# Boundary to the expert tiles laid out anew: batch 7's scans ahead of other routing, batch 4 scattered first, two tiles multiplied ahead of the last output

## The reference

```python
x = _layernorm(x + rwkv(x))            # time mixing, three projections, scans over time, Wo
x = _layernorm(x + moe(x))             # 8 experts, the 2 best of each token, F = 176
x = _layernorm(x + linear_attention(x))
x = _layernorm(x + ternary_ffn(x))     # hidden size 704

# moe
router_logits = x_flat @ gate_w.T
top_w, sel = jax.lax.top_k(router_logits, 2)
top_w = jax.nn.softmax(top_w, axis=-1)
h = silu(x_e @ gate_proj.T) * (x_e @ up_proj.T)
out = sum over the two experts of top_w * (h @ down_proj.T)
```

## Time and profile before

| | |
|---|---|
| median of 3 executions | 408.02 us (407.43 to 408.28) |
| the profiled execution's own time | 407.56 us |
| its span | 405.7 us |
| PE busy | 365.0 us, 90% of the span, 2426 matmuls |
| PE weight loads busy | 325.6 us (80%) |
| DVE / ACT / POOL busy | 292.5 (72%) / 210.9 (52%) / 139.3 (34%) us |
| mean granted clock of PE | 0.959 |

### The profile page before, as it was taken

The page is one execution under the profiler, slowest core; times in us unless marked ns, Lnnn a source line. Parts: engine busy times, 40 slices in busy tenths (PEclk is TensorE's granted clock), DMA queues, the critical chain, the costliest instruction groups (busy, mean ns, idle before and its releaser), DMA issues.

```text
span 405.7 us, 7764 instructions
## 1 busy us (share of the span) xinstructions
PE 365.0 (90%) x2426; PEld 325.6 (80%) x2426; DVE 292.5 (72%) x747; ACT 210.9 (52%) x484; POOL 139.3 (34%) x234
## 2 busy tenths in 40 slices
PE   6999999999558999999999868899999999999791
PEld 6999889999436876777777656899999999999680
DVE  5699999999964556797543255687979787886642
ACT  7256686677634333355335322656565645645451
POOL 2001077767765510003211076525344340411111
PEclk9999999999769999999999986999999999999987
DMA  7879611111024457433441132102020200000000
GB/s 221 314 242 177 225 59 40 53 54 53 15 93 129 135 204 225 136 108 92 126 134 44 64 90 65 53 2 78 3 79 0 79 27 2 27 1 27 0 27 26
DMA packets 28567, 35.79 MB, mean 88 GB/s; under 512 B 3696, under 2 KB 25712, under 8 KB 28272
## 3 DMA queue, kind: packets, MB, share of 16 engines
q1 hardware_dynamic: 19696, 21.78, 18.5%
q0 software_dynamic: 3072, 8.39, 6.4%
q10 hardware_dynamic: 5760, 5.12, 3.8%
HBM read 22.83 MB, written 12.45 MB: 87 GB/s over the span
## 4 chain that ended last, share of the span: by engine, by line
PE 42%; DVE 33%; issue 8%; ACT 5%; POOL 5%; DMA 4%; SPq 2%; ACTq 0%; POOLq 0%; DVEq 0%
PE bank L413 12%; PE bank L556 10%; PE bank L577 8%; DVE st L1102 4%; PE bank L745 2%; PE bank L690 2%; PE bank L536 2%; PE bank L566 2%; PE bank L423 2%; DVE arena L1185 2%; DVE arena L1163 2%; DVE arena L1574 2%; DVE arena L1567 2%; DMA arena<-in_xT 2%; DVE arena L1476 1%
## 5 line engine op out<-in xcount | busy, mean ns | idle before, releaser
L807 ACT ACTIVATE arena<-bank 128x256 f32<-128x256 f32 (+1 forms) x118 | 45.3, 422 | 43.9 <-PE bank L577 28.4
L1663 POOL TENSOR_TENSOR ve<-mv,eps 128x2 f32<-128x2 f32 x32 | 7.7, 240 | 159.8 <-DVE mv L1106 106.9
L556 PE MATMUL bank<-gu,arena 128*128 x156 | 54.0, 469 | 0.0
L812 ACT ACTIVATE arena<-arena,nm,rs 128x256 f32<-128x256 f32 x48 | 26.2, 596 | 38.5 <-POOL nm L1671 38.4
L1741 POOL DMA_INDIRECT arena<-yg,ypos x32 | 31.1, 973 | 39.0 <-DMA yg<-arena 30.5
L577 PE MATMUL bank<-dn,arena 96*128 x156 | 41.0, 385 | 3.3 <-DVE arena L1352 3.3
L1715 POOL DMA_INDIRECT xg<-x,pos x32 | 36.6, 1145 | 13.8 <-issue 7.3
L1352 DVE COPY arena<-bank 96x256 f32<-96x256 f32 x39 | 16.3, 419 | 34.2 <-PE bank L566 33.8
L577 PEld LDWEIGHTS bank<-dn,arena 96*128 96x128 f32 x156 | 28.7, 190 | 13.1 <-issue 5.0
L413 PE MATMUL bank<-arena 128*128 128x256 f32 (+2 forms) x192 | 34.4, 322 | 4.4 <-ACT arena L807 3.6
L413 PE MATMUL bank<-x_hi,w1q 128*128 128x256 f32 x128 | 36.0, 305 | 1.5 <-ACT x_hi L807 1.5
(11 more groups left out here) (274 smaller groups left out, 1121.7 us busy)
## 6 DMA issues: line engine op xcount, KB each, us to landing
arena<-xg SPq DMA_DIRECT2D x39, 128.0 KB, 2.2
yg<-arena ACTq DMA_DIRECT2D x39, 128.0 KB, 1.7
arena<-in_xT SPq DMA_DIRECT2D x8, 256.0 KB, 5.3
x<-in_x SPq DMA_DIRECT2D x8, 256.0 KB, 4.4
out<-arena SPq DMA_DIRECT2D x8, 256.0 KB, 2.1
gu<-in_w_gate SPq DMA_DIRECT2D x1, 1408.0 KB, 9.2
gu<-in_w_up SPq DMA_DIRECT2D x1, 1408.0 KB, 8.4
dn<-in_w_down SPq DMA_DIRECT2D x11, 128.0 KB, 5.4
```

What stands on the lines that cost most here:

```text
L556: last = pe.matmul(bank[BANK_GU[i % 2]][:, 0:2 * F], xtT[:, i % 2, chunk(k)], w[:, :, k, :, bass.ds(e, 1), :], start=k == 0, stop=k == KC - 1)
L807: return act.activation(dst, src, ACT.Copy)
L812: last = act.activation(dst[:, t, :], src[:, t, :], ACT.Identity, bias=nm[:, i, t:t + 1], scale=rs[:, i, t:t + 1])
```

## The change

It moves work at the boundary on every engine, adds one small DVE instruction in place of a POOL one, and computes batch 5's weights another way. Cut to its core:

```diff
-GATED = B - 2
+GATED = B - 3
 # SP
+            sp.wait_ge(mv_ok[0], B - 2)
             sp.wait_ge(table_ok, 1)
 # PE, a_slot
                 if 0 <= now < B - 1:
                     output(now)
+                if old == FULL_AT - 1:
+                    rank(old)
+                    first_total()
                 if 0 <= new < B:
                     past(pe, gate_ok, new)
                     project(new, 2, halves(3), rp_mm)
-                if 0 <= old < B:
+                if 0 <= old < FULL_AT - 1:
                     rank(old)
-                    if old == FULL_AT - 1:
-                        first_total()
 # PE, boundary
             tile_order(0, bank[7][:, 4 * E:4 * E + 1])
-            turn_x1(B - 3)
-            logits(B - 3)
             tile_rows(0, bank[7][:, 8 * E:8 * E + 2 * FIRST], where1[:, :, :])
             output(B - 2)
-            rank(B - 3)
+            turn_x1(B - 3)
             for i in range(3):
                 experts[i] = expert_of(i)
             turn(0)
+            logits(B - 3)
             turn(1)
             gate_up(0, experts[0])
             turn(2)
+            gate_up(1, experts[1])
+            rank(B - 3)
+            output(B - 1)
+            turn(3)
+            tile(0)
             turn_x1(B - 2)
-            output(B - 1)
+            tile_front(1)
             logits(B - 2)
-            gate_up(1, experts[1])
-            turn(3)
-            tile_front(0)
-            rank(B - 2)
-            tile_back(0)
-            turn_x1(B - 1)
-            tile_front(1)
-            logits(B - 1)
             tile_back(1)
             tile_front(2)
+            rank(B - 2)
+            tile_back(2)
+            turn_x1(B - 1)
+            tile_front(3)
+            logits(B - 1)
+            tile_back(3)
+            tile_front(4)
             rank(B - 1)
...
 # ACT: a_slot leaves out normalise_x1(5); boundary
             exponents_high(B - 1)
+            gate_exponentials(B - 1)
+            normalise_x1(B - 3)
             copy_x1T(B - 3)
-            gate_exponentials(B - 1)
-            odds(B - 3)
             turned(0)
+            turned(1)
             reciprocal(B - 1)
             act.preload_act_table_set("silu_and_others")
-            turned(1)
-            normalise_x1(B - 2)
             turned(2)
-            copy_x1T(B - 2)
             silu(0)
             silu(1)
+            turned(3)
+            gaps(B - 3)
+            normalise_x1(B - 2)
+            tile(0)
+            copy_x1T(B - 2)
+            tile(1)
             gaps(B - 2)
-            turned(3)
+            tile(2)
             normalise_x1(B - 1)
-            tile(0)
             copy_x1T(B - 1)
-            tile(1)
+            tile(3)
             gaps(B - 1)
-            tile(2)
-            tile(3)
 # DVE, a_slot
                     residual(now)
+                if old == FULL_AT - 1:
+                    positions(old)
+                    dve.wait_ge(pos_ok, old)
+                    dve.wait_ge(route_step, 4 * old + 4)
+                    dve.tensor_copy(pos[:, tiles_of(old), :], pos_f[:, tiles_of(old), :]).then_inc(pos_ok, 1)
+                    first_places()
                 outputs(s)
-                if 0 <= old:
+                if 0 <= old < FULL_AT - 1:
                     positions(old)
 # DVE, boundary
             exponents(B - 1)
-            finish_y(B - 2)
             dve.wait_ge(asked_ok, valid_at[0])
             tile_places(0, where1, bank[7][:, 4 * E:4 * E + 1])
+            differences(B - 1)
+            tile_table(0, bank[7][:, 8 * E:8 * E + 2 * FIRST])
+            finish_y(B - 2)
             states(B - 1)
-            tile_table(0, bank[7][:, 8 * E:8 * E + 2 * FIRST])
+            outputs(B - 1)
             choose(B - 3)
-            residual(B - 2)
-            outputs(B - 1)
-            positions(B - 3)
 # POOL
             for s in range(B + 2):
+                if s - 2 == FULL_AT - 1:
+                    scatter(s - 2)
+                    deviation(0, s)
+                    weights(s - 2)
+                    continue
```

More of the change, by code:

```diff
@@ L626, in _ @@
             pe.matmul(bank[5][:, 0:E], ones[:, :], taken_e[:, :], start=True, stop=True).then_inc(looked_ok, 1)
-            tile_back(2)
-            tile_front(3)
+            tile_back(4)
+            tile_front(5)
             tile_order(1, bank[6][:, 0:1])
-            tile_back(3)
-            tile_front(4)
+            tile_back(5)
+            tile_front(6)
             tile_rows(1, bank[6][:, 8 * E:8 * E + 2 * SECOND], where2[:, :, :])
-            tile_back(4)
+            tile_back(6)
             def turn_x2(b):
@@ L640, in turn_x2 @@
                 transposes(x2[b % 2], halves(BANK_TURN)).then_inc(x2Tp_ok, 1)
-            for i in range(5, TILES):
+            for i in range(7, TILES):
                 tile_front(i)
@@ L925, in a_slot @@
                     odds(old)
-                if 0 <= now:
+                if 0 <= now < B - 3:
                     normalise_x1(now)
@@ L1164, in exponents, with differences @@
                                        ALU.max).then_inc(wkv_step, 1)
+            def differences(s):
                 dve.wait_ge(wkv_step, 4 * s + 2)
@@ L1274, in pairs @@
                                          ALU.add).then_inc(pair_step, 1)
-            def a_slot(s):
-                old, now = s - 2, s - 1
-                exponents(s)
-                if 0 <= now:
-                    finish_y(now)
-                if s == 0:
-                    xs_low(1)
-                if s + 2 < B:
-                    xs_low(s + 2)
-                states(s)
-                if 0 <= old:
-                    choose(old)
-                if 0 <= now:
-                    residual(now)
-                outputs(s)
-                if 0 <= old:
-                    positions(old)
             def tile_counts(j, counts):
@@ L1316, in tile_table, with first_places, a_slot @@
                                 found.rearrange("p (q i) -> p q i", q=2)).then_inc(table_ok, 1)
+            def first_places():
+                dve.wait_ge(total_ok, 1)
+                dve.wait_ge(pair_step, pairs_at)
+                tile_counts(0, bank[6][:, 0:E])
+                dve.tensor_tensor(valid[:, 0:1], count[:, 0:1], lev1[:, :], ALU.is_ge).then_inc(asked_ok, 1)
+            def a_slot(s):
+                old, now = s - 2, s - 1
+                exponents(s)
+                differences(s)
+                if 0 <= now:
+                    finish_y(now)
+                if s == 0:
+                    xs_low(1)
+                if s + 2 < B:
+                    xs_low(s + 2)
+                states(s)
+                if 0 <= old:
+                    choose(old)
+                if 0 <= now:
+                    residual(now)
+                if old == FULL_AT - 1:
[4 more added lines that the diff above has]
+                    first_places()
+                outputs(s)
+                if 0 <= old < FULL_AT - 1:
+                    positions(old)
             for s in range(B - 1):
@@ L1326, in _ @@
                     dve.memset(pick[64:65, :].bitcast(F32), 1.0).then_inc(rows_ok, 1)
-            dve.wait_ge(total_ok, 1)
-            dve.wait_ge(pair_step, pairs_at)
-            tile_counts(0, bank[6][:, 0:E])
-            dve.tensor_tensor(valid[:, 0:1], count[:, 0:1], lev1[:, :], ALU.is_ge).then_inc(asked_ok, 1)
             exponents(B - 1)
-            finish_y(B - 2)
             dve.wait_ge(asked_ok, valid_at[0])
             tile_places(0, where1, bank[7][:, 4 * E:4 * E + 1])
+            differences(B - 1)
+            tile_table(0, bank[7][:, 8 * E:8 * E + 2 * FIRST])
+            finish_y(B - 2)
             states(B - 1)
-            tile_table(0, bank[7][:, 8 * E:8 * E + 2 * FIRST])
+            outputs(B - 1)
             choose(B - 3)
-            residual(B - 2)
-            outputs(B - 1)
-            positions(B - 3)
             def hidden(i):
@@ L1485, in _ @@
             finish_y(B - 1)
-            residual(B - 1)
-            hidden(0)
-            choose(B - 2)
-            hidden(1)
-            positions(B - 2)
-            hidden_turned(0)
+            residual(B - 2)
+            hidden(0)
+            positions(B - 3)
+            hidden_turned(0)
+            hidden(1)
+            residual(B - 1)
             dve.scalar_tensor_tensor(taken[:, :], order[:, 0:1], float(FIRST), valid[:, 0:1], ALU.is_lt,
@@ L1497, in _ @@
             hidden(2)
-            choose(B - 1)
+            choose(B - 2)
             hidden_turned(2)
             hidden(3)
+            positions(B - 2)
+            hidden_turned(3)
+            hidden(4)
+            choose(B - 1)
+            hidden_turned(4)
+            hidden(5)
             positions(B - 1)
@@ L1511, in _ @@
             dve.tensor_copy(done[:, :], bank[5][:, 0:E])
-            hidden_turned(3)
-            hidden(4)
+            hidden_turned(5)
+            hidden(6)
             tile_places(1, where2, bank[6][:, 0:1])
```

(8 more changed lines are left out.)

5 lines of the change are left out of this document (3 added, 2 removed).

## The result

| | before | changed |
|---|---|---|
| median | 408.15 us (407.43 to 409.33, 4 runs) | 403.56 us (403.14 to 403.99, 4 runs) |
| ratio, 95% interval | | 0.9885 (0.9857 to 0.9912) |
| profiled execution, span | 407.56, 405.7 us | 403.19, 401.1 us |
| mean granted clock of PE | 0.959 | 0.968 |

The kernel is 4.6 us faster, 5.8 were forecast (402.2).

What follows compares the result with a forecast made beforehand. POOL's queue, and behind it a DVE to PE chain, was taken as the bound before the tiles. Terms -5.0 - 1.92 - 0.91 + 0.36 + 1.65 = -5.8 us gave 401.7, forecast 402.2 for the median, range 400.7 to 405.0.

Steps and rivals of the forecast that it cites:

- Scatter and load: POOL and SP, batch 4: first scatter at 101.65 instead of 107.55, first load issued at 110.25 instead of 116.14.
- batch 4's scatter becomes slow: Rival, chance 0.09: beside outputs(6) and exponents(7) all four scatters take 1.95, the start slips 0.7, total 402.9 us.
- Start of the tiles: PE's first expert product starts at 114.9 against 119.92, minus 5.0 us, with a cold output(6) of 3.34.
- Cold product and wait gone: PE's first tiles: low clock and short wait at first product and turn(2) go, -1.92; wait before down(0) goes, -0.91.
- The new wait: PE at turn_x1(7) waits 1.65 us for ACT's normalise_x1(7), which stands behind evacuate(2), turned(6) and store(2).
- output(7): PE's output of batch 7: finish_y(7) is done at 117.2, PE reaches it at 117.8, so it hides by 0.6.
- Behind, as long as before: The stages behind the tiles take as long as before, with no wait at turn(13).
- The cover at turn(13): Second batch of loads: load 13 is there by 150.9, turn(13) at 152.1; margin 1.2 us where it was about 4.
- slower than before: Rival, chance 0.05: clearings at 2.2 us each add 9.4, PE starves at turn(13) one for one past the margin: 410.4.
- The clock stays up: Rival, chance 0.12: PE's clock holds through the pause at 103.6, output(6) takes half, everything 1.2 earlier: 401.0 us.
- Clock down longer: Rival, chance 0.12: PE's clock stays low as logits(5) waits for its copy, through the first product: 404.2 us.
- nothing happens: Rival, chance 0.02: the first load waits for something else than the scatters: 408.0 us.

Runs made afterwards that it cites:

- second pair of profiles: Kernel before and changed kernel, each profiled again from a later set of runs, edits unchanged; last 32 products took 6.12 us before, 6.61 changed.
- combined kernel: Changed kernel plus ACT's normalise_x1(7) ahead of tile 2's copies and 2 and 5 idle products around the last turn_x3: 400.78 us, ratio 0.9834.
- executions above 410: Three of six executions of the unedited changed kernel, rerun beside the kernel before; median 406.72 us, ratio 0.9895 from the three near 403; none above 410 profiled.
- first set: Changed kernel rerun without edits on another chip, against the kernel before at 411.07 us: 410.46 us (12 runs), ratio 1.0002.

## Why the prediction was right, and where it was off

The forecast was 402.2 (400.7 to 405.0); 403.56 came. Its steps, in its own terms:

- *Scatter and load.* First scatter 101.65 said, 101.61 measured. First load 110.25 said, 109.25 measured. The scatters keep their usual spacing (the last began 3.93 after the first, not 5.15: the long ones of the earlier trace rows ran beside DVE's scans of `states`). By the same row the rival *batch 4's scatter becomes slow* fell: the longest took 1.10, although DVE ran five instructions with two SBUF inputs in a row beside them, from 101.85 to 105.60, the last a scan. With the old order, beside the two scans of `states(7)`, they took 1.42 and 1.25. The rule behind the rival is that of the Trainium skill (SBUF — State Buffer, section "SBUF: two separate sides"): a DVE instruction with two SBUF inputs and a GpSimd instruction that reads SBUF take turns at one port pair. The scatters in their new place don't bear it out; the 1.93 us of POOL's small multiplication beside three subtractions of DVE, in the kernel with POOL's old order, would fit it. Why `states` lengthens a scatter and the scan at 104.38 doesn't is open.
- *Start of the tiles.* 114.9 said, 115.11 measured, -4.81 for -5.0. The cold output took 3.78 for 3.34. `turn(0)` came at 113.70, not at the 113.0 where the forecast's chain had it: it follows batch 5's norm (111.28) by 2.42, and the three reads of the table in that time are a term that the sum left out. The transposes, the copy and `logits(5)` hid it, so that the start came close partly by luck.
- *Cold product and wait gone*: -1.92 and -0.91, as said; the product takes 1.35 and `down(0)` has no wait. *rank(5)* +0.36, as said (117.70 to 118.06).
- *The new wait*: 1.65 said, 1.75 measured (the terms given, 1.82 - 1.09 + 1.08 less a tenth of the norm, make 1.70), removed by moving the norm, as the theory has it.
- *output(7)*: y(7) was said to be ready 0.6 before PE asks. It was (117.60, and PE was there at some 118.1), but the output also needs the bank that `residual(6)` reads (L1258), and that step was left out of the count: the add ends at 118.20 and the output begins at 118.34, some 0.3 late. In the kernel with the output first the same add ends at 119.30, and the output begins at 119.44. With this the terms make about -5.3 at `down(6)`, as measured (5.35), where 5.8 had been said.
- *Behind, as long as before*: this is the step that failed. The tiles kept the 5.3 us to their last `down` (224.01 against 229.30), block three added 0.4 (254.51 against 260.23 at the product of L745, now L750), and the last piece gave back 1.10, because the low clock took a longer stretch of it. So of the 1.2 us by which the gain in the span fell short (4.6 for 5.8) 0.5 lie ahead of `down(6)` and 0.7 behind it. With the second pair of profiles the last piece gives back 0.5 only (6.61 against 6.12). The combined kernel shows that the last piece is a matter of the clock, worth up to 2.5 us.
- *The cover at turn(13)*: margin 1.2 said, 1.1 measured; two more clearings brought on just the loss of the rival 'slower than before', and at two us for each us of waiting, not one for one, since the clock falls in the wait. The rival's price was too low; its condition wasn't met in the profiles of the changed kernel. Whether it was met in the executions above 410 is not known.
- *The clock stays up*: it did not (0.50 at `output(6)`). With idle products `turn(0)` came no earlier, so the rival's 1.2 us at the start was too much; by the estimate above it is 0.3. *Clock down longer*, *nothing happens*: not seen in the first comparison; the ratio of 1.0002 in the first set is 'nothing' by another road, since there the first load and the start of the tiles did come early.

## What to carry to other kernels

A boundary between two stages is a knot of queues: pulling one thread (the scatter) made it 8 us slower, and undoing another by itself cost 8 or 9, while all together gained 4.6. So such a change is predicted queue by queue, asking at each moved step who stands behind it. A pause on PE can be paid twice, once as itself and once as low clock behind it; a few idle products in front of the last dense piece kept the clock up there, and in front of `output(6)`, where another engine sets the next step, they made that step no earlier. Compare a change in more than one set of executions: this one gained 1.1% in two comparisons, with three executions of six left out of one of them, and nothing in a third. And when a change pulls a stage forward, measure the cover of the transfers behind it: here 4.05 us became 1.1, which a normal variation of a DMA's landing (1.4 or 3.3 us) can use up.

## What the runs showed of the hardware

- SP's wait for the same eight clearings was 1.4 us in some profiles and up to 3.3 us in others; in the one looked at, by nine late packets.
- After PE's stand of 3.08 us at `turn(13)`, or in its pauses before and its 1.85 ahead of the output put first, its clock was at 0.50; after one of 0.67 at `turn(13)` it was at 1.00. The same 1.75 before x1(7) left the clock up in the changed kernel's first profile (product behind it 1.35) and brought it down in that of the first set (2.56), where PE had stood 1.33 three us before, but also with POOL's old order (2.55), where no such stand was near.
- POOL's `topw<-topw,gap` on 128x2 took 0.20, 0.59 or 1.93 us, the last beside three subtractions of DVE.
- On one of the three chips DVE and ACT stood for 2.3 to 3.8 us at the same two places for PE results that were there, and the whole gain of the change was gone. That the one made the other is not shown: on another chip three of six executions lost as much, unseen.
